# Attention and MoE layer on one core: attention sums passed through DRAM, row maxima sent per partition half, values laid out in blocks

## The chip, the cores and the metric

One core of a Trainium2 chip runs the whole program in one launch. The metric is the device time of one execution in microseconds (us); lower is better. The kernel before was timed in three executions, and one of them was profiled.

## The reference

The input `x` is 16 batches of 512 rows of 256 numbers, all in float32. The layer adds three things: the input itself, attention, and a mixture of experts, both computed from the normalised rows.

```python
def _L0_attn_ref(x, ...):                      # 16 heads of 16 numbers, window of 128 keys
    q = (x @ Wq.T + bq).reshape(B, S, N_HEADS, D_K)      # k and v alike
    scores = jnp.einsum('bqhd,bkhd->bhqk', q, k) * SCALE
    scores = jnp.where(mask, scores, jnp.float32(-10000.0))
    attn = jax.nn.softmax(scores, axis=-1) + jnp.float32(1e-09)
    ctx = jnp.einsum('bhqk,bkhd->bqhd', attn, v).reshape(B, S, D_MODEL)
    return ctx @ Wo.T + bo

def _L0_ffn_ref(x, ...):                       # 8 experts, 2 per row, and a shared one
    ...
    combined = jnp.einsum('beh,be->bh', eo, c)
    ...
    return (combined + shared_out).reshape(B0, S0, H0)

xn = _layernorm(x, axis=-1)
x = x + _L0_attn_ref(xn, ...) + _L0_ffn_ref(xn, ...)
```

## The kernel before

The program has five stages with a barrier of all engines between them: rows are normalised and their gate values computed; the routing is worked out; queries, keys and values are projected and stored to DRAM (`q_d`, `k_d`, `v_d`), and the rows sorted by expert; the expert blocks run; and last the attention stage, whose functions begin with `b_`, does the attention, the shared expert, the output projection and the final sum. Products of float32 are made of three products of rounded parts (`PASSES`): a number is split in a "hi" part and the remainder "lo", so most operands exist twice.

In the projection stage the values of a batch are written by VectorE into `q_v` (line 715), in which every value is followed by a one, so that a row of `v_d` is value, 1, value, 1 and so on. `q_gpsimd` sets the ones once (line 605), and line 721 reads the values back for a total.

**The attention stage.** `turns` runs 18 turns: turn t works on the scores of batch t, and on later steps of the batches t-1 and t-2. The turns 2 to 14 are a loop. Each turn has 16 slots (`for h in range(H)`); what an engine does in a slot is written out in its function `turn`, and each engine works through its own list in order. The 16 slots of scores of a batch are 4 head groups of 4 slots. `LAG_...` numbers say how many slots after the scores a step comes. The helpers `due`, `due_group` and `due_chunk` turn a lag into the batch, the group, or the chunk of two groups, whose step is due in a slot.

For a group g the steps are these:

- `load_qk` on the sync engine (SP) loads its queries and keys in eight DMAs (lines 811 and 813), four slots ahead of its scores, once the transposed scores of the batch before no longer need the place.
- `scores` on TensorE (PE, line 1227) and `masked_max` on VectorE (DVE, line 1462) give the row maxima; `turn_maxima` transposes them; ScalarE (ACT, `maxima_hi`, line 1350) and VectorE (`maxima_lo`, line 1471) split them in hi and lo; and both parts go by DMA into two rows of `b_q`, at the partitions 48 and 112, or 49 and 113. Both DMAs are issued by ACT (line 1355): the hi part in `maxima_hi`, the lo part at the end of the same slot (`maxima_lo_out`).
- `scores_t` (line 1250) is the second product, 8 slots after the scores, in which these rows subtract the maxima. It waits for both DMAs. `exponentials` (ACT, line 1369) follows, and GpSimd (POOL, lines 1150 and 1152) clears what the mask hides.
- `values` (line 1267), 14 slots after, multiplies with the values and ones: even partitions of the result are sums of values, odd ones are denominators. `copy_sums` (ACT, line 1376) takes them to `b_u`.
- `move_sums` (SP) moves them inside SBUF after each group: one DMA takes one denominator row of each head, at every 32nd partition, into 32 rows of `b_zc` (line 1104), and one takes the even partitions into `b_uc` (line 1105).

```python
            def move_sums(b, g):
                c, at = g // 2, 32 * (g % 2)
                hold(sp, b_ue, 4 * b + g + 1)
                ...
                sp.dma_start(b_zc[at:at + 32, c, :], b_u[1:P:32, g % 2, :]).then_inc(b_zl[g % 2], 16)
                sp.dma_start(b_uc[2 * at:2 * at + 64, c, :], b_u[0:P:2, g % 2, :]).then_inc(b_ul[g % 2], 16)
```

For a chunk c of two groups `reciprocals` (DVE, line 1490), a store of them to `rz_d` (SP, line 1109), a load that spreads each over 16 partitions (SP, line 1113), `normalise` (POOL, line 1160), `context_hi` (ACT, lines 1381 and 1383) and `context_lo` (POOL, line 1164) follow.

Between these steps stands the shared expert. PE multiplies gate and up parts in the slots 8 to 15 (line 148), ACT and DVE make the hidden values (lines 1388, 1477, 1484), POOL their remainders (`hidden_lo`, line 1169, in the slots 11, 13, 15 and 1 of the next turn), and PE projects them in the slots 2 to 5. `project_context` adds the attention part in the slots 6 and 7, and `finish` (DVE, line 1501) the rest in the slots 7 and 8. POOL gathers the experts' rows (line 1177), ACT scales them (line 1412), and ACT stores the result in slot 9. SP loads values (line 1096), rows for the shared expert (line 1136, slot 8) and the residual input (line 1140, slot 10).

`hold` and `after` are waits on a semaphore. The sync engine waits and issues in the order written: a DMA behind a wait leaves late, whatever it is.

## Time and profile before

| | |
|---|---|
| median of 3 executions | 2066.18 us |
| lowest, highest | 2057.62 us, 2073.88 us |
| the profiled execution | 2073.88 us, span 2071.9 us |
| mean granted clock of TensorE in it | 0.902 of full speed |
| busy share of the span: PE, DVE, ACT, POOL | 83%, 54%, 44%, 39% |
| bytes moved by DMA | 333.80 MB, mean 161 GB/s |
| the attention stage | from 1206 us to the end |
| the reciprocals of a second chunk are spread at | 1500.67, 1551.66, 1603.45 and 1652.71 us, a turn apart |

The profiled execution was the slowest of the three, 0.4% above the median, so a time worked out on its trace is carried over to the median by the same difference. The span is the time between the first and the last instruction in the trace. Busy time of one engine says little by itself: engines work beside each other, and what counts is who is waited for last.

### The profile page before, as it was taken

The page shows a single profiled execution, that of the slowest core. Times are in us where ns is not written, and L with a number is a line of the kernel's source. Part 1 is how long each engine was busy: PE and PEld are TensorE (multiplying, and loading weights), DVE is VectorE, ACT ScalarE, POOL GpSimd, SP SyncE. Part 2 cuts the span into 40 slices and gives each one's busy share as a digit, 9 for nine tenths or more (in the row PEclk, how much of TensorE's full clock was granted, in tenths as well). Part 3 has the DMA queues.
Part 4 walks back from the last instruction along what each step waited for, and adds up shares of the span by engine and source line. Part 5 has one row for each costly group of instructions (what it writes and reads, how often), then busy time and mean ns, then how long its engine had stood idle before and what let it go on. Part 6 is the DMA issues. An engine that isn't in the chain of part 4 may idle for free.

```text
span 2071.9 us, 38865 instructions
## 1 busy us (share of the span) xinstructions
PE 1728.1 (83%) x11609; PEld 1421.9 (69%) x11610; DVE 1129.1 (54%) x3465; ACT 905.9 (44%) x1737; POOL 808.9 (39%) x757
## 2 busy tenths in 40 slices
PE   6936545550999999999999988889899999899987
PEld 6925535540888888888888865666666666666666
DVE  6653232331666666666666665565565655555552
ACT  2312111111555554545455435555555655555553
POOL 0024332340000000000000026788788888888886
PEclk9998777775999999999999968899888998998998
DMA  8447766765444444444444447666677767777752
GB/s 281 141 146 220 226 208 203 221 212 191 148 147 147 145 149 151 152 152 152 152 152 152 129 102 146 145 161 154 146 157 153 166 158 160 152 160 154 155 125 75
DMA packets 254491, 333.80 MB, mean 161 GB/s; under 512 B 26992, under 2 KB 172656, under 8 KB 252400
## 3 DMA queue, kind: packets, MB, share of 16 engines
q1 hardware_dynamic: 202368, 261.44, 46.3%
q0 software_dynamic: 12288, 33.57, 6.5%
q10 hardware_dynamic: 39792, 38.28, 5.5%
q8 instruction: 20, 0.33, 0.1%
q14 instruction: 23, 0.19, 0.0%
HBM read 210.52 MB, written 112.72 MB: 156 GB/s over the span
## 4 chain that ended last, share of the span: by engine, by line
PE 54%; SPq 14%; issue 12%; DMA 10%; POOL 4%; ACT 3%; DVE 2%; another core or an unknown queue 0%; ACTq 0%; POOLq 0%; DVEq 0%
PE psum L148 31%; PE psum L783 11%; SPq L576 7%; DMA plain_arena<-xn_d 4%; DMA split_arena<-k_d 4%; PE psum L1227 4%; PE psum L1267 2%; PE psum L1250 2%; SPq L811 2%; PE psum L854 2%; SPq L813 2%; ACT plain_arena L1369 1%; POOL split_arena L1169 1%; POOL plain_arena L1152 1%; DMA plain_arena<-y_d,b_ix 1%
## 5 line engine op out<-in xcount | busy, mean ns | idle before, releaser
L148 PE MATMUL psum<-split_arena 128*128 128x512 f32 (+1 forms) x4560 | 996.0, 374 | 20.4 <-POOL split_arena L1169 10.8
L148 PEld LDWEIGHTS psum<-split_arena 128*128 128x128 f32 x4560 | 787.4, 201 | 159.3 <-POOL split_arena L1169 17.0
L1462 DVE CUSTOM_DVE_ANT_0 plain_arena<-psum,mask 128x256 f32<-128x256 f32 (+1 forms) x1024 | 340.2, 386 | 306.0 <-PE psum L1227 276.8
L1369 ACT ACTIVATE plain_arena<-psum 128x512 f32<-128x512 f32 (+1 forms) x512 | 250.8, 543 | 322.4 <-PE psum L1250 282.9
L1212 POOL MEMSET plain_arena<- 128x256 f32 x1 | 0.3, 312 | 699.0 <-ACTq L137 699.0
L783 PE MATMUL psum<-split_arena 128*128 128x256 f32 x1872 | 233.8, 285 | 0.0
L1227 PE MATMUL psum<-split_arena 48*128 48x256 f32 (+1 forms) x1024 | 169.8, 356 | 70.1 <-DMA split_arena<-k_d 44.9
L783 PEld LDWEIGHTS psum<-split_arena 128*128 128x128 f32 x1872 | 226.9, 192 | 0.1
L1227 PEld LDWEIGHTS psum<-split_arena 48*128 48x128 f32 x1024 | 106.1, 205 | 149.3 <-issue 71.8
L613 POOL DMA_INDIRECT sorted_d<-plain_arena,q_idx x128 | 124.2, 970 | 206.1 <-DVE q_idx L700 170.4
L900 ACT ACTIVATE plain_arena<-psum 128x512 f32<-128x512 f32 x156 | 93.3, 598 | 219.3 <-PE psum L148 219.1
L926 DVE TENSOR_TENSOR split_arena<-plain_arena,split_arena 128x1024 fp32r<-128x1024 f32 x117 | 143.4, 1226 | 57.7 <-ACT split_arena L881 57.6
L951 DVE TENSOR_TENSOR plain_arena<-psum,plain_arena 128x512 f32<-128x512 f32 x156 | 107.8, 691 | 117.0 <-ACT plain_arena L900 113.9
L1150 POOL TENSOR_SCALAR_AFFINE_SELECT plain_arena<-plain_arena 128x1024 f32<-128x1024 f32 x128 | 140.3, 1096 | 36.9 <-ACT plain_arena L1369 35.8
L626 PE MATMUL psum<-ident,plain_arena 128*128 128x128 f32 x128 | 28.7, 398 | 145.2 <-DMA plain_arena<-xn_d 128.8
L881 ACT CAST split_arena<-plain_arena 128x1024 fp32r<-128x1024 f32 x117 | 122.7, 1049 | 45.3 <-DMA plain_arena<-in_gate_w 42.2
L1152 POOL TENSOR_SCALAR_AFFINE_SELECT plain_arena<-plain_arena 128x1024 f32<-128x1024 f32 x128 | 139.9, 1093 | 0.0
L1267 PE MATMUL psum<-plain_arena 128*32 128x256 f32 (+1 forms) x2048 | 134.7, 411 | 3.1 <-issue 2.8
L1177 POOL DMA_INDIRECT plain_arena<-y_d,b_ix x128 | 122.5, 957 | 25.4 <-issue 20.7
L1250 PE MATMUL psum<-split_arena 50*128 50x256 f32 (+1 forms) x1024 | 120.1, 296 | 9.1 <-issue 5.9
L626 PEld LDWEIGHTS psum<-ident,plain_arena 128*128 128x128 f32 x128 | 23.3, 208 | 151.6 <-DMA plain_arena<-xn_d 110.4
L677 ACT ACTIVATE split_arena<-psum,bqk 128x512 fp32r<-128x512 f32 x64 | 39.6, 687 | 188.0 <-DMA k_d<-split_arena 105.8
(132 smaller groups left out, 1946.7 us busy)
## 6 DMA issues: line engine op xcount, KB each, us to landing
plain_arena<-in_gate_w SPq DMA_DIRECT2D x39, 512.0 KB, 5.1
plain_arena<-in_up_w SPq DMA_DIRECT2D x39, 512.0 KB, 6.2
plain_arena<-in_down_w SPq DMA_DIRECT2D x39, 512.0 KB, 7.0
plain_arena<-sorted_d SPq DMA_DIRECT2D x39, 512.0 KB, 3.9
y_d<-plain_arena ACTq DMA_DIRECT2D x39, 512.0 KB, 3.6
plain_arena<-in_x SPq DMA_DIRECT2D x32, 512.0 KB, 3.9
plain_arena<-xn_d SPq DMA_DIRECT2D x32, 512.0 KB
q_d<-split_arena SPq DMA_DIRECT2D x64, 256.0 KB
```

The source lines that it names most:

```text
L148: last = pe.matmul(out, lhs_t(p), rhs(q), start=(begins and c == 0 and k == 0), stop=(ends and c == len(chunks) - 1 and k == 2), skip_grou ...
L576: sp.dma_start(dram[ds(b, 1), m * 2 * HG:(m + 1) * 2 * HG, part, :, :].rearrange("o h d s -> (o h) d s"), q_qk[:, u, k, part, m, :].bitcas ...
L613: pool.indirect_dma_start(sorted_d, bass.IndirectOffsetOnAxis(q_idx[:, u, a, n:n + 1], 0), q_x[:, u, a, :], None).then_inc(q_sc[u], 16)
L783: last = pe.matmul(psum[:, 6 + a // 2, (a % 2) * D:(a % 2 + 1) * D], h(p, m, a), w(q, 2, m * D, D), start=(first and k == 0 and a % 2 == 0 ...
L926: dve.tensor_tensor(c_w[:, v, 1, n, :], c_raw[:, n, :], c_w[:, v, 0, n, :].bitcast(F32), ALU.subtract).then_inc(c_wlo, 1)
L1150: pool.affine_select(out=v[:, 0:16:2, :], in_=v[:, 0:16:2, :], compare_op=ALU.is_ge, fill=0.0, base=0, pattern=[[0, 8], [1, P]], channel_m ...
L1152: pool.affine_select(out=v[:, 1:16:2, :], in_=v[:, 1:16:2, :], compare_op=ALU.is_ge, fill=0.0, base=0, pattern=[[0, 8], [-1, P]], channel_ ...
L1227: last = pe.matmul(psum[:, par, (i % 2) * 2 * P:(i % 2) * 2 * P + cols], b_q[rows, g, p, i * P:(i + 1) * P], b_k[rows, g, p, (i + 1) * P - ...
L1250: last = pe.matmul(psum[:, 2 + par, (j % 2) * 2 * P:(j % 2) * 2 * P + cols], b_k[rows, g, p, j * P:(j + 1) * P], b_q[rows, g, p, j * P:j * ...
L1267: last = pe.matmul(psum[32 * r:32 * r + 32, 4, j * P:(j + n) * P], b_v[:, s, j, 32 * r:32 * r + 32], b_pt[:, s, r, 2 * j:2 * j + n, :], st ...
L1369: act.activation(b_pt[:, g % 2, 2 * p + par, 4 * half:4 * half + n, :].rearrange("p k s -> p (k s)"), psum[:, 2 + par, 0:n * P], ACT.Exp, ...
L1462: last = dve.tensor_tensor_reduce(b_junk[:, 2 * par + i % 2, 0:cols], psum[:, par, at:at + cols], mask[:, 2 * P - cols:2 * P], -1.0, 3e38, ...
```

## The change

It touches four things.

*The layout of the values.* A head has 16 values and then 16 ones, instead of values and ones in turn. The sums of a head so come out in 16 partitions and its denominators in the 16 behind.

*The way of the sums.* `move_sums` is gone. After both groups of a chunk, `store_sums` writes all of `b_u` to a new DRAM tensor `u_d` (512 KB), one slot later than the second group's copy, and `load_sums`, again a slot later, waits until it is complete and loads the denominators and the sums from there. The lags behind it are shifted: the reciprocals come in slot 7 and 15 instead of 5 and 13, their store in the same slot 7 and 15, their spreading in slot 8 and 0 instead of 7 and 15, the product on POOL in slot 10 and 2 instead of 9 and 1, and both context steps a slot later as well.

*The maxima.* Each part goes in two DMAs, one for each partition, instead of one. The lo part's are issued by SP, first of all in its slot (`load_maxima_lo`, slots 6, 10, 14 and 2), and no more by ACT.

*Semaphores* follow from these.

```diff
         rz_d = nc.dram_tensor("rz_d", (2, 2 * HG, S), F32).ap()
+        u_d = nc.dram_tensor("u_d", (2, 2, P, S), F32).ap()
...
-        q_v = plain_take(2, T, H, DH, 2)
+        q_v = plain_take(2, T, H, 2, DH)
...
-                    dve.tensor_tensor(q_v[:, u, 2 * h:2 * h + 2, :, :, 0],
+                    dve.tensor_tensor(q_v[:, u, 2 * h:2 * h + 2, :, 0, :],
...
-        LAG_RC, LAG_RS, LAG_SP, LAG_N, LAG_CH, LAG_CL = 17, 18, 19, 21, 22, 23
+        LAG_US, LAG_UL, LAG_RC, LAG_SP, LAG_N, LAG_CH, LAG_CL = 16, 17, 19, 20, 22, 23, 24
...
-            def move_sums(b, g):
-                c, at = g // 2, 32 * (g % 2)
-                hold(sp, b_ue, 4 * b + g + 1)
-                if g % 2 == 0:
-                    hold_after(sp, b_uz, 2 * b + c - 1)
-                sp.dma_start(b_zc[at:at + 32, c, :], b_u[1:P:32, g % 2, :]).then_inc(b_zl[g % 2], 16)
-                sp.dma_start(b_uc[2 * at:2 * at + 64, c, :], b_u[0:P:2, g % 2, :]).then_inc(b_ul[g % 2], 16)
+            def load_maxima_lo(b, g):
+                hold(sp, b_nlo, 4 * b + g + 1)
+                for par in range(2):
+                    row = 64 * par + 49
+                    sp.dma_start(b_q[row:row + 1, g, :, :].rearrange("w p s -> w (p s)").bitcast(F32),
+                                 b_m[8 * par:8 * par + 8, g % 2, 1, :].bitcast(F32)).then_inc(b_ldl[g % 2], 16)
+
+            def store_sums(b, c):
+                hold(sp, b_ue, 4 * b + 2 * c + 2)
+                hold_after(sp, b_uz, 2 * b + c - 1)
+                sp.dma_start(u_d[c, :, :, :].rearrange("g p s -> p g s"), b_u[:, :, :]).then_inc(b_us, 16)
+
+            def load_sums(b, c):
+                hold(sp, b_us, 16 * (2 * b + c) + 16)
+                rows = u_d[c, :, :, :].rearrange("g (r w d) s -> w (g r) d s", w=2, d=DH)
+                sp.dma_start(b_zc[0:64, c, :], rows[1, :, 0, :].rearrange("h (k s) -> h k s", s=64)).then_inc(b_zl[c], 16)
+                sp.dma_start(b_uc[:, c, :], rows[0, :, :, :]).then_inc(b_ul[c], 16)
...
-                load_maxima(b, g, 0).then_inc(b_ldm[g % 2], 16)
-
-            def load_maxima(b, g, w):
-                return act.dma_start(b_q[48 + w:P:64, g, :, :].rearrange("q p s -> q (p s)").bitcast(F32),
-                                     b_m[0:16, g % 2, w, :].bitcast(F32))
-
-            def maxima_lo_out(b, g):
-                act.wait_ge(b_nlo, 4 * b + g + 1)
-                load_maxima(b, g, 1).then_inc(b_ldl[g % 2], 16)
+                for par in range(2):
+                    row = 64 * par + 48
+                    act.dma_start(b_q[row:row + 1, g, :, :].rearrange("w p s -> w (p s)").bitcast(F32),
+                                  b_m[8 * par:8 * par + 8, g % 2, 0, :].bitcast(F32)).then_inc(b_ldm[g % 2], 16)
```

On the sync engine the slots 7 and 8 of a turn in the loop read like this before. L1109 stores the reciprocals of the first chunk (it is the step of slot 6), L1104 and L1105 move sums, L1113 spreads the reciprocals, L1096 loads values, L811 and L813 are queries and keys (the other half of them follows):

```order
L1109 DMA rz_d<-plain_arena 64x64 [waits b_reciprocal]
L119 REGISTER_ALU
L1104 DMA plain_arena<-plain_arena 32x1x64 [waits b_sums_copied,b_normalised]
L1105 DMA plain_arena<-plain_arena 64x512
L119 ISA
L1113 DMA plain_arena<-rz_d 128x1x512 [waits b_reciprocal_stored]
L119 ISA
L1096 REGISTER_ALU [waits b_values_summed]
L1096 DMA plain_arena<-v_d 128x4x128
L811 ISA [waits b_scores_transposed]
L811 DMA split_arena<-q_d 16x2x512
L813 DMA split_arena<-q_d 32x2x512
```

And this is the same stretch of the changed kernel, from the second load of slot 5 on. L1105 is now a DMA of the lo maxima, L1121 stores the reciprocals, L1098 loads values, L812 and L814 are queries and keys:

```order
L1117 DMA plain_arena<-u_d 128x1x512
L120 ISA
L1105 DMA split_arena<-split_arena 1x8x128 [waits b_maxima_lo]
L1105 DMA split_arena<-split_arena 1x8x128
L120 REGISTER_ALU
L1121 DMA rz_d<-plain_arena 64x64 [waits b_reciprocal]
L120 REGISTER_ALU
L1098 REGISTER_ALU [waits b_values_summed]
L1098 DMA plain_arena<-v_d 128x4x128
L812 ISA [waits b_scores_transposed]
L812 DMA split_arena<-q_d 16x2x512
```

The moves are gone from it, the lo maxima have come in, and the spreading (now L1125) has gone behind the queries and keys, ahead of the rows for the shared expert and the lo maxima of the next group:

```order
L814 DMA split_arena<-k_d 32x2x512
L1125 DMA plain_arena<-rz_d 128x1x512 [waits b_reciprocal_stored]
L120 REGISTER_ALU
L1154 ISA [waits b_rows_transposed]
L1154 DMA plain_arena<-xn_d 128x4x256
L120 REGISTER_ALU
L1105 DMA split_arena<-split_arena 1x8x128 [waits b_maxima_lo]
L1105 DMA split_arena<-split_arena 1x8x128
L120 REGISTER_ALU
L1158 ISA [waits b_result_stored]
L1158 DMA plain_arena<-in_x 128x4x256
```

On VectorE this is the end of a turn in the loop before. L1462 are the maxima of slot 15, L1477 is a step of the shared expert:

```order
L1462 ISA plain_arena<-psum,mask 128x256
L1462 ISA plain_arena 128x1
L1477 SCALAR_TENSOR_TENSOR plain_arena<-plain_arena,psum 128x512 [waits b_hidden,b_silu]
L1056 REGISTER_ALU
L1056 COMPARE_AND_BRANCH
```

In the changed kernel the reciprocals of the second chunk (L1497) stand between that step (L1485) and the branch, behind which the maxima of slot 0 follow; before, they stood two slots earlier:

```order
L1470 ISA plain_arena<-psum,mask 128x256
L1470 ISA plain_arena 128x1
L1485 SCALAR_TENSOR_TENSOR plain_arena<-plain_arena,psum 128x512 [waits b_hidden,b_silu]
L126 REGISTER_ALU [waits b_denominators_loaded1]
L1497 RECIPROCAL plain_arena<-plain_arena 64x64 [waits b_reciprocal_stored]
L1058 REGISTER_ALU
L1058 COMPARE_AND_BRANCH
```

## Rows read from the trace of the kernel before

**Rows 1.** The page: busy tenths of TensorE in 40 slices of the span.

```profile
PE   6936545550999999999999988889899999899987
```

**Rows 2.** Waits of PE, 1250 to 1950 us: us in total, times, longest.

```profile
PE psum L1227 <- DMA split_arena<-k_d: 40.8, 17, 4.6
...
PE psum L148 <- POOL split_arena L1169: 5.6, 10, 1.4
```

**Rows 3.** Timeline of PE: start us, us, instructions [idle before them <- releaser].

```profile
1533.46 1.66 PE L148 MATMUL psum<-split_arena 128*128 128x512 f32 x6
1537.94 0.60 PE L1227 MATMUL psum<-split_arena 48*128 48x128 f32 x4 [2.82 <-DMA split_arena<-k_d]
...
1538.77 2.02 PE L148 MATMUL psum<-split_arena 128*128 128x512 f32 x6
...
1541.32 0.53 PE L1250 MATMUL psum<-split_arena 50*128 50x256 f32 x4
...
1550.76 0.51 PE L1250 MATMUL psum<-split_arena 50*128 50x256 f32 x4
...
1590.12 0.51 PE L1250 MATMUL psum<-split_arena 50*128 50x256 f32 x4 [1.40 <-issue]
```

**Rows 4.** Timeline of the sync engine's DMA issues.

```profile
1525.78 0.64 SPq L1113 DMA_DIRECT2D plain_arena<-rz_d  x1
...
1527.65 0.41 SPq L811 DMA_DIRECT2D split_arena<-q_d  x1
...
1531.96 0.43 SPq L813 DMA_DIRECT2D split_arena<-k_d  x1
...
1534.59 0.39 SPq L1140 DMA_DIRECT2D plain_arena<-in_x  x1
...
1540.91 0.38 SPq L813 DMA_DIRECT2D split_arena<-k_d  x1
```

**Rows 5.** Windows: us, busy by engine, granted clock, DMA share, GB/s.

```profile
1500.00:1551.00 51.00, 47.07 (x392) 34.37 (x388) 30.39 (x147) 29.15 (x67) 42.15 (x38) 0.90 0.72 157
1528.00:1546.00 18.00, 15.18 (x126) 10.34 (x128) 11.21 (x54) 11.37 (x25) 14.42 (x13) 0.91 1.10 237
1546.00:1548.00 2.00, 2.00 (x22) 1.18 (x10) 0.77 (x2) 0.46 (x2) 2.00 (x3) 1.00 0.40 102
```

**Rows 6.** Timeline of VectorE.

```profile
1524.24 0.69 DVE L1501 TENSOR_TENSOR plain_arena<-psum,plain_arena 128x512 f32<-128x512 f32 x1
...
1543.87 0.54 DVE L1490 RECIPROCAL plain_arena<-plain_arena 64x64 f32<-64x64 f32 x1
...
1551.25 0.29 DVE L1462 CUSTOM_DVE_ANT_0 plain_arena<-psum,mask 128x128 f32<-128x128 f32 x1
```

**Rows 7.** Timeline of GpSimd.

```profile
1530.10 1.28 POOL L1160 TENSOR_TENSOR plain_arena<-plain_arena 128x512 f32<-128x512 f32 x1 [2.95 <-DMA plain_arena<-rz_d]
...
1542.18 1.29 POOL L1184 TENSOR_TENSOR plain_arena<-plain_arena,bo_sb 128x512 f32<-128x512 f32 x1 [0.60 <-DMA plain_arena<-in_x]
```

**Rows 8.** Timeline of ScalarE and its DMA issues.

```profile
1531.42 0.72 ACT L1381 ACTIVATE plain_arena<-plain_arena,b_vt 128x512 f32<-128x512 f32 x1 [0.64 <-POOL plain_arena L1160]
...
1551.75 1.10 ACT L1369 ACTIVATE plain_arena<-psum 128x512 f32<-128x512 f32 x2
...
1583.71 0.52 ACTq L1355 DMA_DIRECT2D split_arena<-split_arena  x1
```

**Rows 9.** The source line L811: its DMAs from issue to landing.

```profile
DMA to landing us min/median/max: 2.0/4.5/8.4
```

**Rows 10.** Source lines L715 and L951: ns min/median/max.

```profile
L715 DVE TENSOR_TENSOR plain_arena<-psum,bv_sb x32: 681/692/693, 154.7 to 467.4; 128x512 f32<-128x512 f32 x32
...
L951 DVE TENSOR_TENSOR plain_arena<-psum,plain_arena x156: 683/692/694, 521.3 to 1196.0; 128x512 f32<-128x512 f32 x156
```

**Rows 11.** Timeline of PE at the program's end.

```profile
2043.57 8.01 PE L148 MATMUL psum<-split_arena 128*128 128x512 f32 x24 [3.97 <-DVE plain_arena L1477]
...
2056.43 11.38 PE L148 MATMUL psum<-split_arena 128*128 128x256 f32 x72 [4.85 <-POOL split_arena L1169]
```

More of the change, by code:

```diff
@@ L1156, in normalise @@
             def normalise(b, c):
-                for s in range(2):
-                    pool.wait_ge(b_ul[s], 16 * (2 * b + c) + 16)
+                pool.wait_ge(b_ul[c], 16 * b + 16)
                 pool.wait_ge(b_zbl[c], 16 * b + 16)
```

40 lines of the change are left out of this document (21 added, 19 removed).

## The prediction

> **What bounds the kernel now.** The page's slices [rows 1] put the attention stage from slice 24 to the end, with TensorE busy nine tenths or more in most of it. So only TensorE's own gaps can be won there. The table of waits for TensorE from 1250 to 1950 us [rows 2] names them: 40.8 us for a load of keys in 17 waits, and 5.6 us for GpSimd's rounding remainders. Then one turn of 16 slots in order of time, 1500 to 1551 us; turns follow each other by 51 us. TensorE finishes slot 11 at 1535.1, cannot begin slot 12 before 1537.94, after 2.82 us of waiting for the keys of the last head group, and stands in slot 0 of the next turn at 1550.76 [rows 3]. The sync engine's queue shows why the keys are late: their eight DMAs go out from 1527.65 to 1532.3, behind the spreading of the reciprocals (1525.78) and the moves of the sums, and the DMA engines are full up to 1546 [rows 4, 5]. Last, the end of the program, where little covers a wait.
>
> **The loads of slots 8 and 12.** Today the moves of slot 7 wait for ScalarE's copy of the sums, and the keys stand behind. In the new order slot 7 holds the store of the reciprocals, one load of values, then the keys. The reciprocal must be done first: VectorE ends its maxima of slot 7 at 1524.24, where the finishing half now follows, and the reciprocal takes 0.54 [rows 6], so the store goes out at 1524.9, the values at 1525.5, the keys from 1526.3 to 1530.6. That is 1.3 us earlier, and 392 KB (the spread of 256 KB, the moves of 136 KB) are no longer ahead, 1.7 us at the rate of the loaded stretch, 1528 to 1546 [rows 5]. The keys land near 1535, in time for slot 12. By itself this would take away 2.8 us a turn, and the slower products behind it.
>
> **What is late next in slot 12.** The transposed scores of slot 12 also need the low part of the maxima of group 1. Its two DMAs now leave on the sync queue behind 768 KB of keys, 256 KB of reciprocals and 512 KB of rows, near 1532.0. What a transfer costs in that place is the row of the residual input: issued at 1534.59, GpSimd still waits for it until 1542.18, 7.6 us [rows 4, 7]. So the maxima land near 1539.6. Before, they left on ScalarE's queue, and the turn after shows that they can be last even there: issued at 1583.71, and TensorE waits until 1590.12 for something that only they fit, 6.4 us [rows 3, 8]. Those scores start today 0.4 us after 1537.94 here, and at 1590.12, one turn of 51 us after 1539.1, there; the new start is 0.5 to 1.3 later, and I take +0.7 us a turn. Bounds: the best landing in the trace is 2.0 us [rows 9], which would leave no wait for the maxima; the worst of 8.4 us gives +1.8. A second wall stands beside it: the spread of the reciprocals now goes out behind the keys, at 1530.6. It took 4.3 us to GpSimd's product (1525.78 to 1530.10 [rows 4, 7]) with a quieter queue, so the product begins at 1534.9 or later and takes 1.28. ScalarE's context step sits behind it (0.72 and a cast of about as much), then two scalings (about 0.5 each) and the exponentials of slot 12 (1.10) [rows 8]. TensorE needs these for the transposed scores of slot 13, which so start at 1539.7 at the earliest, against 1541.32 [rows 3].
>
> The Trainium skill ("DMA: Bandwidth & Descriptors", section "Queues, rings and completion order") says that SP and ACT each own one ring on the same 16 engines, that a ring is consumed in order and that an engine takes turns between rings. By that rule leaving ACT's ring for SP's is what makes the low maxima late; if the ring made no difference, their term would be 0 instead of +0.7. The trace agrees only in that the residual input, deep in SP's ring, took the 7.6 us above. The same page of the Trainium skill (section "Why a DMA increments its semaphore by 16 and not by 1") lets the number of engines follow from the outermost sizes: 2 for the old form of 2x8x128, 8 for the new one of 1x8x128. That would speak for earlier maxima; no row here counts the engines of one DMA.
>
> **The sums' round trip.** Each chunk's sums were moved inside SBUF, one hop after each group. Now they are one store of 512 KB and, after its completion, two loads: 1 MB a turn is added to 8.0 MB (51 us at the turn's rate [rows 5]), and the sync engine stands still for the store. First chunk: the store follows the keys of slot 4, which leave well ahead of slot 7 and into a quiet queue; with the median of 4.5 us for it and 2 to 3 us for the loads I have the denominators there before VectorE wants them at 1524.2. VectorE's first finishing half falls behind the reciprocal, 0.54 us of delay for the gate product of slot 8, and that is absorbed before slot 12. Second chunk: the residual input leaves at 1534.6 as now, the values, then the keys of the next turn until 1540.0 (the last one is issued at 1540.91 now), then the store until 1540.5. With the 7.6 us of that stretch, and with the engines full until about 1546 and quiet after it [rows 5], plus 1.6 us for 376 KB more, it completes near 1548. The denominators leave at 1548.6 and land near 1550.5; the low maxima of group 2 leave at 1550.2 and land 2.0 us later, 1552.2. Slot 0's transposed scores start at 1550.76 today and its exponentials at 1551.75 [rows 3, 8]; with 0.3 us for the first products the exponentials now start at 1552.5, +0.75. The reciprocal, which sat at 1543.87, long before anyone needed VectorE, now is the last thing of slot 15, ahead of the maxima at 1551.25 [rows 6]: +0.54, beside the first. I take +0.7 a turn for both. Bounds: a store of 4.5 us (the median landing of a key load [rows 9]) leaves +0.54; one of 10 us moves everything behind it by 2.4, so +3.1.
>
> **The rest.** GpSimd multiplied the second chunk in slot 1 ahead of the last hidden remainder, for which TensorE waits in slot 2 (the 5.6 us of [rows 2]); the product is now in slot 2, behind it. That gives 5.6 us back; bounds 0 and twice that. ScalarE issues two DMAs of 0.52 us for the high part, [rows 8], instead of one for each part: TensorE's products of slots 6, 10, 14 and 2, where the sums of values lie, cover this; without cover it would be 0.5 us four times a turn. ScalarE also no longer waits for VectorE there. In the projections the value rows are written 16 in a row instead of every second word: both the strided form and an ordinary one from PSUM take 0.69 us [rows 10], 0 it is, with bounds of 0.1 us either way by 48 instructions, 5 us. **The end:** TensorE waits 3.97 us at 2043.57 because the product of chunk 0 waited for its spread and ScalarE stood behind, and at 2056.43 for the last remainder, itself behind a product [rows 11]. No keys are loaded there, so the round trip fits; I take 2.5 + 1.2 = 3.7 us back, bounds 0 and 5.
>
> **Sum.** Slot 12, 14 x 0.7 = +9.8; slots 15 and 0, 14 x 0.7 = +9.8; GpSimd's order, -5.6; the end, -3.7. Together +10.3 us. On the profiled execution (span 2071.9, time 2073.9) this is 2084.2; on the median of 2066.2, 2076.5, which I give. It is +0.5%, and this kernel's three runs differ by 0.8%, so about 1% is what a measurement can tell from no change.
>
> **Rivals.** *The key wait goes and nothing takes its place* (faster). For it: the keys do leave earlier, and the transfers that pass in the quiet parts take 2 to 4.5 us. The wall above leaves 1541.32 - 1539.7 = 1.6 us a turn. The gate products behind the wait take 2.02 us where those ahead take 1.66 [rows 3]; three slots of that are 1.1 us more. Less 0.54 for the reciprocal it is -2.2 x 14 = -31, with -9.3 from the rest -40, 2026. Against it: the 7.6 us and the 6.4 us. *The second store does not fit* (slower). The sync engine is blocked by it; from 8.3 us on, the denominators land after 1551.25, VectorE stands at the end of the loop, and the maxima of slot 0, the low maxima of group 2 and the keys of slot 4 all wait. At 10 us this is 3.1 x 14 = +43, with slot 12's +9.8 and -9.3, 2110. For it: a store of 512 KB behind 768 KB of keys in the busiest stretch; against it: the engines fall quiet after 1546. *The waits only change names* (same): slot 12 at 0, slot 0 at +0.54, the rest as summed: -1.7, so 2064.
>
> **How the numbers follow.** Forecast and the third rival together, which both lie within 1%: 0.38. Round trip or slot 12 worse than taken, by over 1%, beyond 2087: 0.37, a broad set of which the rival at 2110 is the middle. Key wait gone: 0.25. The range reaches from 2032, most of the way to the faster rival, to 2120, above the slower one: store and maxima both at their bad end give (1.8 + 3.1) x 14 - 9.3 = +59, 2125, and I leave the last of it out. The likeliest case alone would be 2058 to 2092.
>
> **What would show it.** In the changed profile: the keys of slot 12 issued some 1.3 us earlier and no 40.8 us group for them; in its place waits of TensorE's transposed scores, without a visible releaser or for the maxima's DMA, of 2 to 4 us in slot 12; in the sync engine's waits a new group for the store of the sums, 5 to 8 us twice a turn; the reciprocal directly ahead of slot 0's maxima. I am wrong if a turn is under 50 us (slot 12 free), or over 53 us, with VectorE waiting for denominators.

## The result, and the profile after

The changed kernel takes 2125.18 us (median of four, 2115.26 to 2129.08), the kernel before beside it 2068.19: ratio 1.0285, 95% interval 1.025 to 1.032. (The ratios in this document are those of the record and can differ a little from the quotient of the two medians, here 1.0276.) The prediction was 2076.5 us, 0.5% slower, and at most 2120. The kernel became 2.9% slower, and the time lies outside that range. The profiled execution took 2118.96 us, span 2116.9.

Which stage is it? The windows of the stages before and after the change (us, then busy time and instructions of TensorE, its weight loads, VectorE, ScalarE and GpSimd, then granted clock, DMA share, GB/s), first of the kernel before:

```profile
500.00:1206.00 706.00, 686.89 (x4056) 610.01 (x4056) 446.86 (x588) 352.98 (x529) 3.51 (x1) 0.99 0.46 149
1250.00:1900.00 650.00, 583.03 (x4843) 425.70 (x4846) 382.00 (x1838) 365.67 (x818) 527.92 (x477) 0.91 0.71 157
```

and of the changed kernel, with the row of the source line that writes the values:

```profile
500.00:1206.00 706.00, 690.12 (x4066) 612.40 (x4066) 449.45 (x603) 353.17 (x529) 4.72 (x3) 0.99 0.46 150
1250.00:1900.00 650.00, 545.51 (x4524) 397.04 (x4528) 358.32 (x1730) 344.32 (x768) 495.36 (x447) 0.89 0.69 164
L716 DVE TENSOR_TENSOR plain_arena<-psum,bv_sb x32: 681/692/693, 156.3 to 465.4; 128x512 f32<-128x512 f32 x32
```

Up to 1206 us nothing has changed, and the write of the values in blocks takes the same 692 ns as [rows 10]. In 650 us of the attention stage TensorE gets through 4524 products instead of 4843. Its busy time over the whole program is the same (page: 1724.3 us, before 1728.1), and so is the mean of a product in this window (120.6 ns, before 120.4): it waits more, 104.5 us of the 650 against 67.0. For what, says the table of waits, 1250 to 1950 us (us in total, times, longest), to be read beside [rows 2]; the lines of TensorE, GpSimd, ScalarE and the sync engine:

```profile
PE psum L1267 <- issue: 34.9, 15, 3.2
PE psum L1267 <- DMA split_arena<-split_arena: 29.7, 13, 3.6
PE psum L1244 <- DMA split_arena<-k_d: 19.0, 12, 2.7
PE psum L1284 <- DVE split_arena L1501: 11.8, 9, 1.5
PE psum L1267 <- ACT plain_arena L1381: 9.4, 12, 0.9
...
POOL plain_arena L1177 <- DMA plain_arena<-rz_d: 111.5, 25, 8.9
...
ACT plain_arena L1392 <- POOL plain_arena L1177: 49.6, 19, 4.9
ACT b_vt L1416 <- POOL split_arena L1181: 14.8, 9, 2.2
...
SPq L121 <- DMA u_d<-plain_arena: 133.2, 20, 9.2
```

L1267 are the transposed scores, L1284 the values, L1177 GpSimd's product with the reciprocals, L1392 ScalarE's context step. The wait for keys has been halved (40.8 us before). Of the two groups above it the wait for the maxima's DMA is new, and the one without a releaser was 5.9 us before. Off TensorE two walls have grown: GpSimd stood 45.8 us in 23 waits for the spread reciprocals before, and 111.5 us in 25 now; ScalarE stood 19.5 us behind GpSimd's product, and 49.6 now. Last, the sync engine waits for its own store, and ScalarE for GpSimd's low context before it may stage totals in `b_vt`.

One turn shows how these hang together. Slot 7's transposed scores start 9.69 us later in this trace than in the other (1532.20 against 1522.51), so times of [rows 3 to 8] are to be shifted by that. The sync engine's issues:

```profile
1540.88 0.64 SPq L814 DMA_DIRECT2D split_arena<-k_d  x1
1541.63 0.65 SPq L1125 DMA_DIRECT2D plain_arena<-rz_d  x1
1542.64 0.39 SPq L1154 DMA_DIRECT2D plain_arena<-xn_d  x1
1543.23 1.38 SPq L1105 DMA_DIRECT2D split_arena<-split_arena  x2
...
1550.49 0.40 SPq L1111 DMA_DIRECT2D u_d<-plain_arena  x1
1559.72 0.65 SPq L1116 DMA_DIRECT2D plain_arena<-u_d  x1
1560.41 0.58 SPq L1117 DMA_DIRECT2D plain_arena<-u_d  x1
1561.19 1.39 SPq L1105 DMA_DIRECT2D split_arena<-split_arena  x2
```

TensorE's timeline in it (start us, us, then in brackets the idle time before it and its releaser); L149 are products of the shared expert, L1244 scores, L1267 transposed scores:

```profile
1543.47 1.66 PE L149 MATMUL psum<-split_arena 128*128 128x512 f32 x6
1546.95 0.60 PE L1244 MATMUL psum<-split_arena 48*128 48x128 f32 x4 [1.82 <-DMA split_arena<-k_d]
1550.35 0.73 PE L1267 MATMUL psum<-split_arena 50*128 50x256 f32 x4 [2.80 <-issue]
1551.01 2.93 PE L149 MATMUL psum<-split_arena 128*128 128x512 f32 x6
1554.21 0.34 PE L1267 MATMUL psum<-split_arena 50*128 50x256 f32 x4
1565.07 0.50 PE L1267 MATMUL psum<-split_arena 50*128 50x256 f32 x4 [2.31 <-DMA split_arena<-split_arena]
```

GpSimd's:

```profile
1548.71 1.27 POOL L1177 TENSOR_TENSOR plain_arena<-plain_arena 128x512 f32<-128x512 f32 x1 [8.12 <-DMA plain_arena<-rz_d]
```

And ScalarE's, the context step and the exponentials of slot 12 behind it:

```profile
1550.01 0.73 ACT L1392 ACTIVATE plain_arena<-plain_arena,b_vt 128x512 f32<-128x512 f32 x1 [4.09 <-POOL plain_arena L1177]
...
1552.10 1.06 ACT L1381 ACTIVATE plain_arena<-psum 128x512 f32<-128x512 f32 x2
```

The spread is issued at 1541.63, and GpSimd can multiply 7.1 us later, where it was 4.3 us [rows 4, 7]. ScalarE, which works in order, stands 4.09 us with the context step at its head; the exponentials of slot 12 stand behind it.

Slot 13's transposed scores start at 1554.21, where the shifted time of before is 1551.01: 3.2 us lost in this turn. The rows say where. The scores of slot 12 start at 1546.95, 0.7 us earlier than the shifted 1547.63, so the keys cost less than before. The transposed scores of slot 12 start at 1550.35; before, they started 0.4 us behind the scores, at 1538.34, which is 1548.03 shifted. That is 2.3 us, and the low maxima, issued at 1543.23, fit the wait of 2.80 us (it has no visible releaser). The other 0.9 us are slower products: the six of L149 behind the two waits take 2.93 us, where the six ahead of them took 1.66. The granted clock from 1551.0 to 1554.2 us is 0.55 of full speed, near the lower of its two levels, 1.2 GHz; before, the same six took 2.02 us, at 0.76. ScalarE's exponentials end at 1553.16, so in this turn TensorE does not wait for the spread's chain; but without the wait for the maxima it would, since 1553.16 is 2.2 us later than the shifted 1551.01. Two walls stand beside each other here, and which one shows is a matter of a microsecond.

The turn is no exception. Over the window, slot 12's transposed scores start 6.9 us behind slot 11's (mean of 12 turns; 5.6 before, mean of 14), and slot 13's 4.0 us behind slot 12's (3.4 before). The six products between the last two take 2.9 us in the mean (2.5 before).

The second chunk's spread does reach TensorE, through slot 5. GpSimd's low context (L1181) is late, ScalarE waits for it before it may stage the totals in `b_vt` (the 14.8 us), VectorE's step behind that (L1501) is late, and TensorE's values wait for it (the 11.8 us). And the second store of the sums is complete 9.2 us after its issue, so the maxima of group 2 leave at 1561.19 and hold slot 0 until 1565.07.

### The profile page after: what moved, and what is told of

Its sections match the earlier page's. It is cut to its first block, busy times and chain, and to the rows that moved or that the text cites. A ratio compares the mean times of both kernels' runs of the same rounds, so it can differ in the third digit from the quotient of the medians.

```text
span 2116.9 us, 39010 instructions
## 1 busy us (share of the span) xinstructions
PE 1724.3 (81%) x11609; PEld 1416.9 (67%) x11610; DVE 1127.5 (53%) x3465; ACT 907.3 (43%) x1737; POOL 811.1 (38%) x757
## 4 chain that ended last, share of the span: by engine, by line
PE 46%; SPq 18%; DMA 17%; issue 13%; DVE 3%; POOL 2%; ACT 1%; DVEq 0%; POOLq 0%; ACTq 0%
PE psum L149 25%; PE psum L784 10%; DMA u_d<-plain_arena 6%; SPq L577 6%; DMA plain_arena<-xn_d 6%; PE psum L1284 3%; SPq L812 3%; SPq L814 2%; PE psum L1244 2%; DMA split_arena<-split_arena 2%; PE psum L1267 2%; PE psum L855 2%; SPq L1105 2%; DMA out<-plain_arena 1%; SPq L580 1%
## 5 line engine op out<-in xcount | busy, mean ns | idle before, releaser
L149 PE MATMUL psum<-split_arena 128*128 128x512 f32 (+1 forms) x4560 | 994.4, 373 | 12.2 <-POOL split_arena L1186 4.9
L149 PEld LDWEIGHTS psum<-split_arena 128*128 128x128 f32 x4560 | 785.0, 200 | 151.4 <-issue 20.0
L1470 DVE CUSTOM_DVE_ANT_0 plain_arena<-psum,mask 128x256 f32<-128x256 f32 (+1 forms) x1024 | 338.5, 386 | 339.8 <-PE psum L1244 339.1
L1267 PE MATMUL psum<-split_arena 50*128 50x256 f32 (+1 forms) x1024 | 121.2, 315 | 88.9 <-issue 42.0
L1244 PE MATMUL psum<-split_arena 48*128 48x256 f32 (+1 forms) x1024 | 154.7, 358 | 33.5 <-DMA split_arena<-k_d 22.7
L1244 PEld LDWEIGHTS psum<-split_arena 48*128 48x128 f32 x1024 | 98.4, 209 | 103.7 <-issue 65.8
L1267 PEld LDWEIGHTS psum<-split_arena 50*128 50x128 f32 x1024 | 93.6, 216 | 103.7 <-issue 78.6
L1284 PE MATMUL psum<-plain_arena 128*32 128x256 f32 (+1 forms) x2048 | 134.8, 413 | 15.8 <-DVE split_arena L1501 15.8
```

The lines of the kernel that those rows point to most:

```text
L149: last = pe.matmul(out, lhs_t(p), rhs(q), start=(begins and c == 0 and k == 0), stop=(ends and c == len(chunks) - 1 and k == 2), skip_grou ...
L1244: last = pe.matmul(psum[:, par, (i % 2) * 2 * P:(i % 2) * 2 * P + cols], b_q[rows, g, p, i * P:(i + 1) * P], b_k[rows, g, p, (i + 1) * P - ...
L1267: last = pe.matmul(psum[:, 2 + par, (j % 2) * 2 * P:(j % 2) * 2 * P + cols], b_k[rows, g, p, j * P:(j + 1) * P], b_q[rows, g, p, j * P:j * ...
L1284: last = pe.matmul(psum[32 * r:32 * r + 32, 4, j * P:(j + n) * P], b_v[:, s, j, 32 * r:32 * r + 32], b_pt[:, s, r, 2 * j:2 * j + n, :], st ...
L1470: last = dve.tensor_tensor_reduce(b_junk[:, 2 * par + i % 2, 0:cols], psum[:, par, at:at + cols], mask[:, 2 * P - cols:2 * P], -1.0, 3e38, ...
```

## Experiments

Every ratio is against the kernel before, timed beside it. In that kernel's own timing the median moved between 2053 and 2068 us from one set to the next, so ratios, not times, are compared.

**One part at a time.** First the changed kernel with the maxima sent as before:

```diff
-                for par in range(2):
-                    row = 64 * par + 48
-                    act.dma_start(b_q[row:row + 1, g, :, :]..., b_m[8 * par:8 * par + 8, g % 2, 0, :]...)
+                load_maxima(b, g, 0).then_inc(b_ldm[g % 2], 16)
...
+                    if b is not None:
+                        maxima_lo_out(b, g)
```

> The changed kernel with the maxima as before: one DMA for each part, both issued by ScalarE. Queue theory (the low maxima are late because the sync queue carries them): most of the 57 us goes, 2070 to 2090 us, and TensorE's 2.3 to 2.8 us waits ahead of the transposed scores of slots 12 and 0 are under 0.7. Round-trip theory (store and loads of the sums block the sync engine and make sums, reciprocals and keys late): the maxima matter little, 2105 to 2125 us.

Measured 2157.97 us, ratio 1.0466 (1.0408 to 1.0524): slower still, outside of both expectations. The new way of sending the maxima is not what makes the change slow, and with the rest of the change in place the old way is worse.

Then the reverse, the kernel before with the changed maxima alone:

> The kernel before with only the maxima changed: two DMAs for each part, the low ones issued by the sync engine first in slots 6, 10, 14 and 2. Queue theory: slot 12 waits for them behind keys and rows, 1 to 2.3 us a turn, 2080 to 2100 us. Round-trip theory: nothing blocks the sync engine for long, 2060 to 2075 us.

2086.38 us, 1.0154 (1.007 to 1.0237), in the range of the queue theory; a later run shows that the split into two DMAs alone costs 1.1%. And only the lags, in the kernel before; the spread so falls behind the keys, and no sums go through DRAM. One wait is added for the sync engine: the low context of the chunk before must be done before new sums come into its place (a run further down has the same wait and loses nothing). The lags:

```diff
-        LAG_RC, LAG_RS, LAG_SP, LAG_N, LAG_CH, LAG_CL = 17, 18, 19, 21, 22, 23
+        LAG_RC, LAG_RS, LAG_SP, LAG_N, LAG_CH, LAG_CL = 19, 19, 20, 22, 23, 24
```

> The kernel before with only the lags of the change (reciprocals in slots 7 and 15, their spread in 8 and 0 behind the keys, product and context steps a slot later); the sums still move inside SBUF. Queue and round-trip theories: within 8 us of the kernel before, perhaps faster by up to 20, since the keys of slot 8 are no longer behind the spread. Lag theory (the reciprocal at the end of slot 15 and the late spread cost by themselves): 2080 to 2095 us.

2144.09 us, 1.0418 (1.0369 to 1.0468), 49 us above the range of the lag theory: the lags alone lose more than the whole change. Its waits, in the same stretch:

```profile
PE psum L1251 <- ACT plain_arena L1370: 30.6, 14, 3.8
...
POOL plain_arena L1161 <- DMA plain_arena<-rz_d: 139.6, 25, 9.5
...
ACT plain_arena L1382 <- POOL plain_arena L1161: 71.7, 22, 5.5
ACT b_vt L1406 <- POOL split_arena L1165: 23.2, 12, 2.3
```

and one turn of it in four timelines, the sync engine first:

```profile
1543.06 0.66 SPq L1114 DMA_DIRECT2D plain_arena<-rz_d  x1
```

then GpSimd:

```profile
1550.10 1.27 POOL L1161 TENSOR_TENSOR plain_arena<-plain_arena 128x512 f32<-128x512 f32 x1 [9.06 <-DMA plain_arena<-rz_d]
```

ScalarE, with the context step and the exponentials behind it:

```profile
1551.41 0.72 ACT L1382 ACTIVATE plain_arena<-plain_arena,b_vt 128x512 f32<-128x512 f32 x1 [5.02 <-POOL plain_arena L1161]
...
1553.50 1.06 ACT L1370 ACTIVATE plain_arena<-psum 128x512 f32<-128x512 f32 x2
```

and TensorE:

```profile
1554.61 0.69 PE L1251 MATMUL psum<-split_arena 50*128 50x256 f32 x4 [2.15 <-ACT plain_arena L1370]
```

Here the chain can be read without a gap: spread, 7.0 us, product 1.27, context step, exponentials, and TensorE, which now names ScalarE. Fourth, the changed kernel with the low maxima issued by ScalarE at the end of its slot, still in two DMAs:

> The changed kernel with its split maxima, but the low ones issued by ScalarE at the end of the slot. Queue theory: as the kernel with the maxima as before, within 8 us of it. Rival (splitting a part in two DMAs, each on one partition, is what costs): within 10 us of the changed kernel, 2115 to 2135 us.

2130.22 us, 1.0333 (1.0284 to 1.0381), not faster than the changed kernel's 1.0285. So taking the low maxima off the sync queue gains nothing. In one turn of this run ScalarE issues them at 1546.89 and 1547.56, and TensorE still stands 2.52 us for slot 12, until 1555.61. From 1250 to 1900 us TensorE is idle for 86.1 us here, against 104.5 in the changed kernel, but a product takes 127 ns in the mean against 121, at a granted clock of 0.86 against 0.89, and that takes the difference back. The rival's range held; what it names, the split, is not shown by it, since the old form was slower still.

**The spread, ahead of the keys.** The same edit in the changed kernel and in the one with the lags alone:

```diff
+                    b, c = due_chunk(t, h, LAG_SP)
+                    if b is not None:
+                        spread_reciprocal(b, c)
                     if h in (0, 4, 8) and valid(t) and not (h == 0 and is_first(t)):
...
-                    b, c = due_chunk(t, h, LAG_SP)
-                    if b is not None:
-                        spread_reciprocal(b, c)
```

> The changed kernel with one thing moved: the spreading of the reciprocals is issued ahead of the queries and keys of slots 8 and 0, not behind them. Order theory (the spread behind 768 KB of keys makes GpSimd's product late, and ScalarE's context step and with it the exponentials stand behind it): GpSimd's 8 us wait of slot 10 falls under 4, 2085 to 2105 us. Round-trip theory (the blocked sync engine is what costs): the keys leave another 2 us later and nothing is gained, 2115 to 2140 us.

> The kernel before with the lags of the change, but the spread ahead of the queries and keys. Order theory: most of the 83 us that the lags alone cost go, 2065 to 2095 us. Rival (the lateness of the steps themselves, reciprocal in slot 15 and context step in slot 4 ahead of ScalarE's staging of the total, costs): 2110 to 2150 us.

The first took 2097.24 us, 1.0204 (1.0133 to 1.0274), where the changed kernel has 1.0285: 0.8%, with intervals that just overlap. The second took 2093.84 us, 1.0188 (1.0122 to 1.0253), where the lags alone have 1.0418: 2.3%, well clear. GpSimd's wait in the first is down from 111.5 us to 17.1, ScalarE's behind it and its wait for the low context are gone, and the 11.8 us of TensorE's values are 0.2. In the second the wait for keys is up instead; its waits, the sync engine's at the end:

```profile
PE psum L1228 <- DMA split_arena<-k_d: 59.5, 16, 5.4
...
POOL plain_arena L1161 <- DMA plain_arena<-rz_d: 57.3, 14, 5.6
...
SPq L120 <- ACT plain_arena L1377: 253.0, 42, 11.2
...
SPq L120 <- DMA rz_d<-plain_arena: 4.6, 9, 1.1
```

The store of the reciprocals and the spread, which has to wait for its landing, now both stand between the moves of the sums and the keys. The wait for the landing is small, 4.6 us in all; issue and landing together put the keys of slots 8 and 0 at 4.4 and 4.5 us behind the move in one turn (1519.00 to 1523.38, 1548.44 to 1552.94), where they were at 3.3 and 3.6 in the kernel before (1524.40 to 1527.65, 1550.30 to 1553.93). What the sync engine mostly stands for is ScalarE's copy of the sums, ahead of the moves. A third kernel put both the spread and the store of the sums ahead of the keys, and a fourth only the store:

> The changed kernel with both the spread of the reciprocals and the store of the sums issued ahead of the queries and keys. Theory 'the second store is late behind 768 KB of keys, and the low maxima of group 2 and VectorE's reciprocal with it' : the store lands 3 to 5 us after its issue instead of 7 to 10, TensorE's waits on the low maxima's DMA fall by half, 2075 to 2090 us (ratio 1.005 to 1.017). Rival 'the store now holds the keys': it waits for ScalarE's copy of the sums in slot 15/7, the keys of slots 4 and 12 leave later, the wait for the keys grows beyond 28 us, 2095 to 2115 us (ratio 1.02 to 1.03).

> The changed kernel with only the store of the sums moved ahead of the queries and keys of slots 4 and 12. Theory 'the late spread decides': the store is no part of that chain, the spread still goes out behind the keys of slots 8 and 0, so the time stays within 1% of the changed kernel, 2110 to 2130 us (ratio 1.025 to 1.033). Rival 'the long second store decides': 2080 to 2100 us (ratio 1.01 to 1.02).

2086.46 us, 1.0163 (1.0117 to 1.0208), and 2115.08 us, 1.0291 (1.024 to 1.0342). The third is in the range of its first theory; its gain over the spread alone (1.0204) is within the intervals. In the fourth, the store alone brings nothing, though the wait for the low maxima's DMA is all but gone (29.7 us before this edit):

```profile
PE psum L1267 <- issue: 33.3, 13, 3.1
PE psum L1244 <- DMA split_arena<-k_d: 19.4, 12, 2.8
PE psum L1244 <- DVE plain_arena L1470: 19.2, 24, 1.6
...
PE psum L1267 <- DMA split_arena<-split_arena: 3.0, 2, 2.7
```

Other waits stand in its place while the late spread is there: those for VectorE's maxima (L1470) were 1.2 us before this edit.

**The maxima and the round trip with that wall away.** The changed kernel with the spread first and the maxima as before:

> The changed kernel with the reciprocals spread ahead of the keys and the maxima sent as before the change (one 2x8x128 DMA per part, both by ACT). It differs from the kernel with shifted lags and the spread first (2093.8 us, ratio 1.019) only by the round trip through DRAM and the layout of the values, and from the changed kernel with the spread first (2097.2, 1.020) only by the maxima. Theory 'late spread hid everything': with it gone, the maxima's split costs what it costs in the kernel before, 19 to 25 us, so this run is 2072 to 2080 us (ratio 1.005 to 1.012) and the round trip is worth -15 us or so. Rival 'the old form suffers from the round trip' (which the pair 2158 against 2130 us suggests): some 28 us slower than with the split, 2115 to 2130 us (ratio 1.03 to 1.04). Third: round trip and form both worth nothing here, 2090 to 2100 us.

2069.93 us, 1.0106 (1.0041 to 1.0172): the first theory's ratio. It differs from the lags with the spread first (1.0188) by the round trip and the layout alone, which so cost nothing there and may give 0.8% (the intervals overlap), and from the changed kernel with the spread first (1.0204) by the maxima alone, which cost 1.0% (these intervals overlap too). From the changed kernel itself it differs by both walls of slot 12, and that is 1.8%, clear of the noise. That sending them in more DMAs costs something whatever the queue shows in the kernel before with the split, all of it on ScalarE:

> The kernel before with only the split: each part of the maxima in two DMAs, all issued by ScalarE. Split theory (two DMAs of one partition each land sooner than one of two partitions, which would explain why the changed kernel got slower by 33 us with the old form): 2040 to 2058 us. Rival (the split itself costs ScalarE 0.5 us an issue and brings nothing): 2060 to 2075 us.

2076.21 us, 1.0106 (1.0039 to 1.0172), a microsecond above the rival's range. ScalarE's two issues for a part take 0.64 us each where one took 0.52 [rows 8]. Two more kernels separate the lags from the round trip:

```diff
-        LAG_US, LAG_UL, LAG_RC, LAG_SP, LAG_N, LAG_CH, LAG_CL = 16, 17, 19, 20, 22, 23, 24
+        LAG_US, LAG_UL, LAG_RC, LAG_SP, LAG_N, LAG_CH, LAG_CL = 16, 17, 18, 19, 21, 22, 23
```

> The changed kernel with the maxima sent as before, and every lag behind the sums' load one slot shorter: reciprocals in slots 6 and 14, spread in slots 7 and 15 (so ahead of the keys without moving any code), product in 9 and 1, context steps as before the change. The round trip through DRAM stays. Theory 'the round trip is harmless, the lags cost': no slower than the kernel before, 2035 to 2060 us (ratio 0.985 to 1.002). Rival 'the round trip does not fit': the load of the second chunk lands after slot 14, VectorE waits for it and holds the maxima; slower than the kernel with the longer lags and the spread first (2069.9 us, 1.011): 2075 to 2100 us (ratio 1.01 to 1.025).

> The kernel before with only the product and both context steps one slot later (slots 10 and 2, 4 and 12 and so on); reciprocals, store and spread stay where they were. Theory 'the sync engine's standing for the store ahead of the keys is what the lags cost': this run has none of that and costs nothing, 2045 to 2065 us (ratio 0.992 to 1.005), and the wait for the last hidden remainder (5.6 us) goes. Rival 'the later context itself costs': ScalarE waits for GpSimd's last remainder and TensorE's sums wait behind it, 2080 to 2095 us (ratio 1.012 to 1.02).

The round trip with shorter lags took 2077.97 us, 1.0127 (1.0064 to 1.019), in the rival's range, and VectorE waits for the denominators (1.5 us with the longer lags, no such wait in the changed kernel):

```profile
DVE plain_arena L1495 <- DMA plain_arena<-u_d: 80.7, 27, 6.5
```

But these waits do not show that the change needs its longer lags. With them, the same kernel takes 1.0106 when the spread is put in front, which the measurements cannot tell from 1.0127, and 1.0466 when it is not: against that the short lags gain 3.4%. This run is also the nearest to the round trip alone: against the kernel before only the round trip, the layout and reciprocals a slot later are new, and they cost 1.3%.

Making only product and context later cost nothing: 2055.7 us, 1.0023 (0.9994 to 1.0053). So what the lags cost with the spread in front, 1.0188, lies in the later reciprocals, store and spread. TensorE's wait for keys accounts for a part of it, 59.5 us there against this:

```profile
PE psum L1228 <- DMA split_arena<-k_d: 45.3, 15, 4.0
```

That is 14 us in the 700 us of the table, of some 34 between the two runs. The rest is not assigned: no run moved the reciprocal on VectorE alone.

**What the kernel before could gain.** Its sync engine stands 175.8 us for ScalarE's copy of the sums, ahead of the moves, and the keys of slots 8 and 0 stand behind them. The move of group 2 goes one slot later, behind the keys, then that of group 0 too:

```diff
                     b, g = due_group(t, h, LAG_U)
-                    if b is not None:
+                    if b is not None and g % 2 == 1:
                         move_sums(b, g)
+                    b, g = due_group(t, h, LAG_U + 1)
+                    if b is not None and g % 2 == 0:
+                        move_sums(b, g)
```

> The kernel before, with the move of group 2's sums issued behind the queries and keys of slot 8; the spread stays ahead of them. If what the sync queue carries ahead of the keys of slot 8 is what makes TensorE wait 2.8 us in slot 12: the keys leave 3 us earlier and 2015 to 2035 us. Rival (the low maxima or ScalarE's context step are late next): 2045 to 2062 us.

> The kernel before with the moves of the sums of groups 0 and 2 both one slot later, behind the queries and keys of slots 0 and 8 (the kernel with group 2's alone: 2029.9 us, ratio 0.990). Theory 'what holds the keys is the wait for ScalarE's copy ahead of them': slot 0's keys leave earlier too, and the time is 2015 to 2035 us (ratio 0.98 to 0.99). Rival 'only slot 12's keys were ever late': no gain over 2030; ratio 0.988 to 0.998.

2029.85 us, 0.9896 (0.9823 to 0.9968), and 2021.88 us, 0.9833 (0.9783 to 0.9883): faster than both kernels of this study (between the two the intervals overlap). TensorE's wait for keys is 12.1 us in the first. The diff is that of the second. TensorE's waits in it:

```profile
PE psum L1253 <- issue: 19.2, 13, 2.1
...
PE psum L1230 <- DMA split_arena<-k_d: 7.0, 7, 1.7
```

and the window, to be read beside the two at the head of the last section:

```profile
1250.00:1900.00 650.00, 604.90 (x5156) 444.65 (x5158) 402.82 (x1950) 385.23 (x866) 557.85 (x504) 0.93 0.74 163
```

A turn is 48.7 us by the spreads (mean of 12; 51.5 in the kernel before, 55.0 in the changed one), and 5156 products pass in the 650 us. TensorE is idle for 45.1 us of them, against 67.0 before, and a product takes 117.3 ns in the mean, against 120.4, at a granted clock of 0.93 against 0.91: fewer waits, and faster products besides. Transfers run as densely as before (0.74 of the engines, 0.71 before): the same bytes allow a faster turn when they are issued in another order.

All runs beside the kernel before:

| Kernel | Time (us) | Ratio |
|---|---|---|
| changed | 2125.18 | 1.0285 |
| changed, maxima as before | 2157.97 | 1.0466 |
| changed, low maxima on ScalarE's queue | 2130.22 | 1.0333 |
| changed, store of the sums first | 2115.08 | 1.0291 |
| changed, spread first | 2097.24 | 1.0204 |
| changed, spread and store first | 2086.46 | 1.0163 |
| changed, maxima as before, short lags | 2077.97 | 1.0127 |
| changed, maxima as before, spread first | 2069.93 | 1.0106 |
| before, lags of the change | 2144.09 | 1.0418 |
| before, these lags, spread first | 2093.84 | 1.0188 |
| before, maxima of the change | 2086.38 | 1.0154 |
| before, maxima split, on ScalarE | 2076.21 | 1.0106 |
| before, product and context a slot later | 2055.70 | 1.0023 |
| before, move of group 2 behind the keys | 2029.85 | 0.9896 |
| before, moves of groups 0 and 2 behind the keys | 2021.88 | 0.9833 |

## Why the prediction was wrong

*Right.* The keys of slot 12 leave at 1536.3 to 1541.5, shifted 1526.6 to 1531.8; I had 1526.3 to 1530.6. The layout costs 0. The low maxima take about the 7.6 us that I took from the residual input: 1543.23 to 1550.35. The last hidden remainder is no longer waited for in the loop (5.6 us), and the run with later product and context alone confirms that the move is free.

*Half right.* The keys were to land near 1535 and not be waited for. They are there at 1546.95, shifted 1537.3: 0.7 us earlier than before and not 2.8, so the wait was halved (40.8 to 19.0 us), not removed. At the end of the program I took 3.7 us back from two waits: the one of 3.97 us is gone, the one of 4.85 us is still there, 4.86. The sign that I named for failure was a turn over 53 us with VectorE waiting for denominators. The turn is 55.0 us, but VectorE has no such group of waits.

*The step that failed: the +0.7 us a turn for slot 12, with the spread's wall at 0.* By slot 13 a turn loses 1.9 us (from slot 11 to 12 1.3, from 12 to 13 0.6), not 0.7, of the 3.5 that it grows by. Three things were wrong in it.

First, the low maxima. Their landing was priced well, but they leave 1.5 us later than the 1532.0 that I had (1543.23, shifted 1533.5), and TensorE starts slot 12 2.3 us late in the turn shown.

Second, the slower products behind a wait, 2.93 us for six. I had counted them for the wait for keys, in the faster rival, and left them out of the term for slot 12.

Third, the second wall: "It took 4.3 us to GpSimd's product (...) with a quieter queue, so the product begins at 1534.9 or later". I saw the chain, wrote "or later", and summed it as 0. The 4.3 us was a landing from ahead of the 768 KB of queries and keys; behind them it was 7.1 here and 7.0 in the kernel with the lags alone. With the 7.6 us that I used for the maxima two sentences earlier, the product would have come at 1538.2 and slot 13 at 1543.0, where 1541.32 and the +0.7 make 1542.0: +1.0 us a turn or +14 us, and 2090 us in all. That is still far from what was measured, and I followed only the first chunk's spread; the second chunk's reaches TensorE through slot 5 (11.8 us), by a path that I had not looked at. The lags with the spread behind the keys cost 4.2%, with it in front 1.9%; in the changed kernel the place of the spread is 0.8%. Since either wall of slot 12 hides the other, moving the maxima's queue gained nothing, and only both together gave 1.8%.

*Mis-sized: slots 15 and 0.* For the store of the second chunk's sums I took 7.6 us, it was 9.2 in this turn (7.3 to 9.7 in the others), between my value and the rival's 10; and the low maxima behind it took 3.9 us from 1561.19, not 2.0. So slot 0 starts 4.6 us late against the shifted 1560.45, 1.4 us more than slot 13 did, and I had 0.7. Of the rival's mechanism this part is there (29.7 us for the low maxima's DMA), the waits of VectorE are not, and as long as the spread is late, moving the store alone brings nothing.

*Not a cost of this order: the reciprocals' new place.* I gave it 0.54 us, and in the changed kernel the keys leave as forecast. But it has a price as soon as the spread is put in front: 1.9% remain with the lags, of which the context's lag is 0.2%. The landing of the store is the least of it (4.6 us).

*Wrong in kind: the maxima.* I charged the low maxima's queue with 0.7 us a turn, and the split with nothing because products cover ScalarE. The queue has no effect that can be measured in the changed kernel (in the kernel before, 1.0154 with the low part on the sync queue and 1.0106 without, with intervals that overlap); the split costs 1.1% in the kernel before, with all of it on ScalarE. The Trainium skill ("DMA: Bandwidth & Descriptors", section "Queues, rings and completion order") has the descriptors of a ring consumed in order; the pair with the low maxima on either queue (1.0285 and 1.0333) shows no gain from leaving the fuller one. The same page of the Trainium skill (section "Why a DMA increments its semaphore by 16 and not by 1") takes the largest number of engines, up to 16, that divides the outermost sizes other than 1 on both sides; by my estimate from it that is two engines for 2x8x128 and eight for 1x8x128. The trace does not settle it: the run that went back to the old form in the changed kernel was slower (1.0466 against 1.0333), but in the kernel before the old form was faster. No run counted the engines.

*Missed:* ScalarE's staging of totals in slot 5 has to wait for the low context of slot 4. With the context early there was no such wait; with only product and context later it is 2.2 us, and with the spread late as well 14.8, which the values of TensorE see as their 11.8 us.

The parts as steps from one kernel to the next: context a slot later, +0.2%; reciprocals, store and spread as in the change but the spread in front, +1.7%; round trip and layout, -0.8%; maxima, +1.0%; spread behind the keys, +0.8%: together the measured +2.9%. Each step is a difference of two ratios, most of them known to about 0.7%, so the steps of 0.8% and 1.0% are not clear of nothing by themselves; only the sum and the larger differences named above are. They also depend on the order in which they are taken: the spread's place is worth 2.3% without the round trip, and the round trip, here -0.8%, costs 1.3% in the run with the short lags.

*Open:* why the old form of the maxima loses 1.3% to the split one where the spread is late, and wins 1.0% where it is not (there against the split form with the low part on the sync queue). GpSimd waits 152.7 us for the spread in the old form and 139.1 in the split one, so it sits in the same wall, but no run says why. A kernel with the old form and the spread late, but the low maxima off ScalarE, was not tried.

## What to carry to other kernels

A landing time belongs to its place in the queue: price a transfer that is moved behind others by a row that stands behind others, and do it for every transfer that moves, not only for the one whose wait is being removed. On an engine that waits in order, look for what stands directly behind a wait: the moves ahead of the key loads wait for ScalarE's copy, and two of them put behind the keys gained 1.7% with no byte less. Follow a late value through each in-order engine to the one that bounds (here DMA, GpSimd, ScalarE, VectorE, TensorE), for every chunk, before calling its term 0. And where two late things end within a microsecond of each other, taking one away shows nothing: test them together too.

## What was not expected of the hardware

Issuing a small DMA for one partition took 0.64 us on ScalarE's queue where the form of two partitions took 0.52. A DMA of 512 KB that was waited for completed after 4.2 us in a quiet place of the turn and after 9.2 in the busy one, in the same trace. Six products that take 1.66 us took 2.93 behind two waits of 1.82 and 2.80 us, at a granted clock of 0.55, so a wait of TensorE cost more than its own length. And with 29.7 us of TensorE's waits for the low maxima removed down to 3.0, the time stayed the same: a total in the table of waits is no gain as long as another chain ends just behind it.
